# Two-layer gated cross-attention: gathers issued a step earlier, buffers zeroed from SyncE, first loads and last lags rearranged

## What is computed

```python
x = x + tanh(g_xattn[l]) * xattn_l(layernorm(x), layernorm(context), mask)
x = x + tanh(g_ffn[l])   * ffn_l(layernorm(x))
...
# layer 0: 8 heads of 64, keys and values from [context, tokens * kv_gate];
#          ffn: top-2 of 8 experts (sparse mixer), 256 -> 512 (gated SiLU) -> 256
# layer 1: 16 heads of 64; ffn: 8-bit rows and ternary weights, 256 -> 1024,
#          depthwise convolution over the tokens (3 taps), SiLU, 1024 -> 256
```

## Time and profile before

| | |
|---|---|
| median of 3 runs | 1635.83 us (1631.14 to 1636.08) |
| profiled execution: its own time, its span | 1635.99 us, 1634.2 us |
| mean granted clock of TensorE | 0.922 of full speed |
| busy share of the span: PE, DVE, ACT, POOL | 80%, 64%, 60%, 68% |
| moved by DMA | 239.96 MB, mean 147 GB/s |

### The profile page before, as it was taken

How to read it: one execution, slowest core, us unless ns; L and a number is a source line. 1 busy time by engine, 2 the same in 40 slices (tenths; PEclk the granted TensorE clock), 3 DMA queues, 4 the chain that set the end, 5 groups by cost and what they waited for, 6 DMA issues and landing times.

```text
span 1634.2 us, 45130 instructions
## 1 busy us (share of the span) xinstructions
PE 1312.6 (80%) x16918; PEld 1009.1 (62%) x16918; DVE 1045.9 (64%) x2819; ACT 987.9 (60%) x2319; POOL 1118.1 (68%) x1365
## 2 busy tenths in 40 slices
PE   1568778768878978879989998888879888888962
PEld 0346555547767766647878786666656666666651
DVE  4368777886556656855656666667666766676753
ACT  2468776655546666654646567667657766776741
POOL 3567876786657765484757677676767676767765
PEclk9788898989989989999999999999999999999975
DMA  4899897387999944377999994353444335434420
GB/s 136 248 173 231 232 188 207 77 213 160 245 217 248 227 88 85 84 195 194 231 239 224 246 252 94 88 92 66 88 88 87 71 88 88 89 68 88 82 50 6
DMA packets 443129, 239.96 MB, mean 147 GB/s; under 512 B 388784, under 2 KB 425760, under 8 KB 434336
## 3 DMA queue, kind: packets, MB, share of 16 engines
q1 hardware_dynamic: 407100, 172.49, 50.8%
q10 hardware_dynamic: 32740, 57.24, 11.5%
q0 software_dynamic: 3072, 7.34, 1.5%
HBM read 107.78 MB, written 35.50 MB: 88 GB/s over the span
## 4 chain that ended last, share of the span: by engine, by line
PE 35%; POOL 21%; DVE 14%; DMA 11%; issue 9%; ACT 3%; SPq 3%; DVEq 2%; ACTq 1%; POOLq 0%
PE bank_ring L1051 9%; POOL probs L623 6%; PE bank_scores L1011 5%; PE bank_out L1070 5%; PE bank_ring L1089 4%; DMA probs_turned<-probs 4%; DMA raw_weights<-moe_results,route_slots 3%; DVE scores L1299 3%; DVE keys L1311 3%; DMA expert_up<-experts_up 3%; PE bank_ring L1037 3%; PE bank_x L1103 2%; PE bank_x L1150 2%; POOL context L683 2%; POOL moe_rows L642 2%
## 5 line engine op out<-in xcount | busy, mean ns | idle before, releaser
L623 POOL TENSOR_TENSOR probs<-scores,probs 112x487 f16<-112x487 f32 x384 | 431.1, 1138 | 298.9 <-ACT probs L822 291.9
L1299 DVE CUSTOM_DVE_ANT_0 scores<-bank_scores,mask 112x487 f32<-112x487 f32 x384 | 239.5, 661 | 216.4 <-PE bank_scores L1011 208.4
L815 ACT ACTIVATE scores<-scores,score_min 112x487 f32<-112x487 f32 x384 | 265.6, 693 | 85.0 <-DVE score_min L1299 81.2
L842 ACT ACTIVATE values<-bank_ring 128x512 f16<-128x512 f32 x192 | 113.8, 593 | 210.2 <-PE bank_out L1070 168.8
L822 ACT ACTIVATE probs<-scores 112x487 f16<-112x487 f32 x384 | 214.2, 604 | 30.3 <-DMA probs_turned<-probs 14.6
L1051 PE MATMUL bank_ring<-weights,kv_B 128*128 128x128 f16 x3072 | 206.6, 227 | 16.1 <-DVE keys L1311 15.4
L1051 PEld LDWEIGHTS bank_ring<-weights,kv_B 128*128 128x128 f16 x3072 | 191.4, 102 | 35.8 <-DVE keys L1311 32.9
L1070 PE MATMUL bank_out<-values,probs_turned 128*128 128x64 f16 x4608 | 177.0, 197 | 30.0 <-issue 15.9
L1070 PEld LDWEIGHTS bank_out<-values,probs_turned 128*128 128x128 f16 x4608 | 164.5, 101 | 34.2 <-issue 19.4
L1316 DVE SCALAR_TENSOR_TENSOR values<-bank_ring,values 128x512 f16<-128x512 f32 x192 | 131.2, 683 | 78.6 <-ACT values L842 78.4
L1037 PE MATMUL bank_ring<-kv_B,weights 128*128 128x488 f16 x768 | 179.1, 369 | 0.4 <-issue 0.4
(11 more groups left out here) (226 smaller groups left out, 2459.1 us busy)
## 6 DMA issues: line engine op xcount, KB each, us to landing
expert_up<-experts_up SPq DMA_DIRECT2D x43, 1024.0 KB
expert_down<-experts_down SPq DMA_DIRECT2D x43, 512.0 KB
raw_weights<-in_weights ACTq DMA_DIRECT2D x8, 1536.0 KB, 10.9
experts_up<-expert_up ACTq DMA_DIRECT2D x8, 1024.0 KB, 4.9
raw_weights<-in_weights ACTq DMA_DIRECT2D x6, 1024.0 KB, 6.4
probs_turned<-probs SPq DMA_TRANSPOSE x384
context_turned_B<-kv_B ACTq DMA_DIRECT2D x16, 375.0 KB, 7.5
kv_B<-context_turned_B ACTq DMA_DIRECT2D x16, 375.0 KB, 4.5
```

The costliest lines, as they stand in the source:

```text
L623: pool.tensor_tensor(PR[:, u % 4, 1, 0:KEYS], S[:, u % 4, 0:KEYS], PR[:, u % 4, 0, 0:KEYS], ALU.subtract).then_inc(probs_split, 1)
L815: act_e.activation(S[:, u % 4, 0:KEYS], S[:, u % 4, 0:KEYS], ACT.Exp, bias=rmin[:, u % 4:u % 4 + 1], scale=-1.0, accum_out=rsum[:, g % 2, ...
L842: act_e.activation(vN[:, j % 2, 0], bank("v", j)[:].rearrange("p (t d) -> p t d", t=4), ACT.Copy, scale=1 / WSCALE).then_inc(v_hi, 1)
L1299: dve.tensor_tensor_reduce(out=S[:, u % 4, 0:KEYS], in0=bS[u % 2][0:TOK, 0:KEYS], in1=mask[:, m, 0:KEYS], scale=1.0, scalar=3.0e38, op0=AL ...
```

## The change

1. `gather(n)` is issued two steps before its `combine`, not one, for all but n = 0 and n = 6.
2. The zeroing moves from ScalarE (step 0) to SyncE (at the start): five DMAs with runs of 5 to 10 KB, from `moe_rows` in SBUF, which VectorE now clears whole. The loads of expert weights move from step 0 to step -3.
3. Context 1 and tokens 1 are loaded by SyncE behind the first six loads; the wait ahead of the load of the other tokens is gone. On VectorE the wait for the gates moves behind `p_apply(0)`, and the eight `split_chunk` from steps -9, -8 to -6, -5.
4. In layer 0 ScalarE rounds the context a step earlier; GpSimd makes the low half of its first part before both `split_probs` of the step, that of its second between them. For n = 0 the layer-1 halves come behind `kv_ready`.
5. The feed-forward steps of sequences 13 to 15 are packed closer, and in the last half of sequence 15 VectorE takes the two taps, the scaling and the rounding beside GpSimd.

The places of the low halves of keys and values behind the masks (L1311, L1316) do not change.

```diff
+ZERO_DMAS = sum(-(-t // XR_SLOTS) for t in TILES)
...
+F_STEPS = {"stats": 13, "rstd": 14, "rows": 15, "round": 16, "turn": 16, "up0": 17, "up1": 18, "sides0": 19,
+           "sides1": 20, "tanh0": 19, "tanh1": 20, "act0": 20, "act1": 21, "max0": 20, "max1": 21, "rate": 22,
+           "scale0": 23, "scale1": 24, "down": 26, "store": 27}
+LAST_HALF = (NSEQ - 1, 1)
+F_QUICK = {"stats": 13, "rstd": 13, "rows": 13, "round": 13, "turn": 13, "up0": 14, "up1": 15, "sides0": 16,
+           "sides1": 17, "tanh0": 16, "tanh1": 17, "act0": 17, "act1": 18, "max0": 17, "max1": 18, "rate": 19,
+           "scale0": 20, "scale1": 21, "down": 22, "store": 23}
...
+def f_step(n, name):
+    return start_b(n) + (F_QUICK if n >= NSEQ - 2 else F_MIDDLE if n == NSEQ - 3 else F_STEPS)[name]
...
@@ sync
-            sp.wait_ge(x_loaded, 16)
-            sp.dma_start(X[:, 1:NSEQ], x_in[1:NSEQ].rearrange("n t d -> t n d")).then_inc(x_loaded, 16)
+            sp.dma_start(ctxb[0:CP, 1], ctx_in[1].rearrange("(t p) d -> p t d", p=CP)).then_inc(ctx_loaded[1], 16)
+            sp.dma_start(X[:, 1], x_in[1]).then_inc(x_loaded[1], 16)
+            sp.dma_start(X[:, 2:NSEQ], x_in[2:NSEQ].rearrange("n t d -> t n d")).then_inc(x_loaded[2], 16)
+            sp.wait_ge(zeros_set, 1)
+            for b in range(2):
+                rows = xs[b].rearrange("(p t) c -> p (t c)", p=128)
+                for at in range(0, TILES[b] * 2 * DIM, XR_SLOTS * 2 * DIM):
+                    n = min(XR_SLOTS * 2 * DIM, TILES[b] * 2 * DIM - at)
+                    sp.dma_start(rows[:, at:at + n], xr[:].rearrange("p s c -> p (s c)")[:, 0:n])\
+                        .then_inc(rows_zeroed, 16)
...
@@ gpsimd
+                if (j + 4) % 4 == 0 and 0 < (j + 4) // 4 < NSEQ:
+                    split_context((j + 4) // 4, 0, 0)
+                if j == -5:
+                    split_context(0, 0, 0)
+                    split_context(0, 1, 0)
+                    split_latents(0, 0)
+                    split_context(0, 0, 1)
+                    split_context(0, 1, 1)
...
                 if is_pair(j):
                     split_probs(2 * j)
...
-                if (j + 4) % 4 == 0 and 0 <= (j + 4) // 4 < NSEQ:
-                    split_context((j + 4) // 4, 0, 0)
+                if (j + 4) % 4 == 0 and 0 < (j + 4) // 4 < NSEQ:
+                    split_context((j + 4) // 4, 1, 0)
                 if is_pair(j):
                     split_probs(2 * j + 1)
-                if (j + 4) % 4 == 0 and 0 <= (j + 4) // 4 < NSEQ:
-                    split_context((j + 4) // 4, 1, 0)
...
-                    if j == combine_step(n) - 1:
+                    if j == combine_step(n) - (1 if n in (BATCHES[0][0], BATCHES[1][0]) else 2):
                         gather(n)
...
@@ scalar
-                if j == 0:
+                if j == -3:
                     act_e.wait_ge(l0_split, L0_CHUNKS)
                     load_raw(2, 0, 6, weights_in, L0_CHUNKS)
                     load_raw(3, 1, 6, weights_in, L0_CHUNKS + MOE_CHUNKS)
-                    act_e.wait_ge(zeros_set, 1)
-                    for b in range(2):
-                        act_e.dma_start(xs[b].rearrange("(t p) c -> p t c", p=128),
-                                        xr[:, XR_SLOTS - 1:XR_SLOTS, :].to_broadcast([128, TILES[b], 2 * DIM]))\
-                            .then_inc(rows_zeroed, 16)
...
-                if j == FIRST_STEP:
-                    load_context(1)
...
+                if (j + 5) % 4 == 0 and 0 <= (j + 5) // 4 < NSEQ:
+                    round_context((j + 5) // 4)
...
@@ vector
-            dve.memset(xr[:, XR_SLOTS - 1], 0.0)
+            dve.memset(xr[:], 0.0)
...
-                if -9 <= j < -7:
-                    for c in range(4 * (j + 9), 4 * (j + 10)):
+                if -6 <= j < -4:
+                    for c in range(4 * (j + 6), 4 * (j + 7)):
                         split_chunk(c)
...
+                    if (n, 1) == LAST_HALF and j == f_step(n, "sides1"):
+                        conv_sides(n, 1)
...
+                    if (n, 1) == LAST_HALF and j == f_step(n, "scale0"):
+                        f_scale(n, 1)
```

130 lines of the change are left out of this document (83 added, 47 removed).

## The result

| | before | with the change |
|---|---|---|
| median of the runs | 1635.95 us (1631.14 to 1638.04, 4 runs) | **1560.62 us** (1556.74 to 1562.03, 4 runs) |
| profiled execution: time, span | 1635.99, 1634.2 us | 1561.87, 1560.1 us |
| mean granted clock | 0.922 | 0.943 |
| busy PE, DVE, ACT, POOL | 80%, 64%, 60%, 68% | 82%, 68%, 63%, 72% |

What follows compares the result with a forecast made beforehand. Bound by VectorE's gather waits with TensorE's half clock behind them, waits for `kv_ready`, and the opening. Rounds 50, other gathers 8, context halves 9, opening 21, end 2: 90 us off 1636 gives 1546 us; range 1519 to 1590.

Steps and rivals of the forecast that it cites:

- Bound, rounds: Sequences 7 to 15: the earlier gather removes VectorE's wait and TensorE's half clock; 50 us gained, bounds 31 and 55.
- The other gathers: Gathers outside those nine rounds, mainly in the expert stage: 8 us gained, bounds 2 and 12.
- Context halves: Layer 0: one context part leaves the path to `kv_ready` each time TensorE waits for it; 9 us, bounds 0 and 16.
- Opening: Start to step 8: earlier first query projection, no zeros issued on ScalarE; 21 us gained, bounds 10 and 28.
- 11.5 again gives 31.7: Opening: context 2, issued at about 20, takes 11.5 us like context 1 and lands at 31.7 us.
- rival B: Opening gives little: context 2 needs 8 us more and turns of steps 0 and 1 wait; 8 of 21 left, 1559; 0.15.
- two parts of layer 1 (3.2 us) leave the path: Opening: GpSimd makes sequence 0's layer-0 halves first, so two layer-1 parts no longer delay the first query projection; 3.2 us.
- End: Last sequences: `f_up(15)` 4.5 us late, VectorE's share takes 8.5 off, statistics cost 2; 2 us gained, bounds -5 and 6.
- the statistics, now in the same step as their use, cost the last pairs some 2 us: End: packing statistics and their use into one step costs the last pairs some 2 us.
- A: Rounds: GpSimd takes over the wait, its late low halves delaying mask or sums; 50 becomes 25, time 1571; chance 0.16.
- C: Every round: the gather's issue on GpSimd becomes the bound; with 8 us each 1650, slower than before; chance 0.03.
- D: Gathers: the change does not do what it says, the gather still late behind the `combine` before it; no chance given.

Runs made afterwards that it cites:

- g_dose: The changed kernel with two idle GpSimd operations of 1.1 us each behind every gather of sequences 7 to 15: 1582.4 us (0.9646).
- z_small: The changed kernel with the zeros issued by SyncE at the same place, but as two DMAs in runs of 1 KB: 1556.5 us (0.952).
- z_old: The changed kernel with the zeroing back on ScalarE in step 0, in its old form, all else as in the change: 1561.2 us (0.9551).
- t_undo: The changed kernel with old step numbers for all feed-forward parts and GpSimd alone on taps, scaling and rounding of the last half: 1551.1 us (0.9458).
- z_late: The changed kernel with SyncE waiting for context 2 before it issues the zeros: 1561.5 us (0.9564).

## Why the prediction was right, and where it was wrong

**Bound, rounds: right.** The wait, its second half at low clock, and their joint price of 6 us per round were read from the earlier trace rows, and 50 us became 47.3 (49.5 and 48.4 by the two runs that set the gather alone). GpSimd's room was rightly called nearly none: `g_dose`. What was missing is that the `combine` does not stay at 1.05 us: it takes 2.42 to 2.44 in eight of the nine rounds, and 2.56 in one. By that the mask is 0.6 us late, and the step takes 7.34 us instead of the 6.72 of the last sequence: 5.6 us in nine rounds. The 0.4 us per round that I took off for GpSimd's crowding stand for another cause, and came near it by luck. The other 1.8 us are of part 5, in the last round. 9 times the mean before, 12.80, less 6.72 is 54.7; less 5.6 and 1.8 that is 47.3.

**The other gathers: right.** 10.8 against 8 forecast, and by the two runs 7.9 and 9.3; over the twelve profiled executions with the early gather the stretch took 394.5 to 401.8 us, so the sizes are not better known than that.

**Context halves: right in kind; the size is met in part by luck.** 10.8 against 9, in a stretch that scatters by 20 us; the wait for `kv_ready` fell by 9.8 (31.7 to 21.9), not below 20 as I had said it would.

**Opening: the step that failed is "11.5 again gives 31.7".** I priced the load of context 2 by that of context 1, which had run beside the tokens. Beside the zeros in large pieces it took 21.8 us. The rule of the Trainium skill that I set against the change ("DMA: Bandwidth & Descriptors", "Queues, rings and completion order") said so, and I had weighted it as the lesser case (rival B, 0.15): B's first half came, context 2 was 10.4 us later than I gave it, but its second half, that the turns of steps 0 and 1 wait too, did not, so 14.3 of 21 us are left and not 8. My own sign of being wrong, context 2 later than 36 us, was there. The 11.5 us were no evidence on this point: the tokens beside which context 1 ran move in packets of 1 KB, as it does itself. A second step was wrong and is hidden in the change: "two parts of layer 1 (3.2 us) leave the path". With context 2 at 30.9 (`z_small`) the first query projection comes at 35.98 and not at 33.5, for VectorE's copy still waits for the first of the two, behind layer-0 parts that had become 4 us longer (`z_old`). That `z_small` has step 0 at 40.6 and step 8 at 100.1, near the 39 and 101 of the forecast, is right in size and not in the chain.

**End: the step that failed is "the statistics, now in the same step as their use, cost the last pairs some 2 us".** The packed steps cost the last pairs 9.4 (27.3 against 17.8 in `t_undo`; 8.7 against the kernel before). I counted the length of the chain, and not what is queued behind its waits: GpSimd's low halves of that step, TensorE's scores of the next, and half clock on top. That `f_up(15)` would be late was right: 5.3 us against 4.5 (from step 191 on 41.9, in the kernel before 36.6). Of the 8.5 us that VectorE's share was to give behind it, 4.9 came. So 8.5 less 4.5 less 2 became 4.9 less 5.3 less 8.7. Scaling and rounding gave 3.5 of 3.9 (7.7 to 4.24 us), but the taps only 1.5 of 4.6, in part since in VectorE's own order `f_act` of the first half stands behind them:

```profile
1538.91 4.28 DVE L1561 SCALAR_TENSOR_TENSOR context<-raw_weights,vectors,context 128x112 f32<-128x112 f32 x8 [1.66 <-ACT context L951]
1543.11 0.62 DVE L1575 SCALAR_TENSOR_TENSOR context<-raw_weights,context 128x448 f32<-128x448 f32 x1
```

GpSimd had the taps of the first half at 1541.67 and ScalarE its tanh at 1542.28; the 0.8 us up to 1543.11 are VectorE's. The `f_act` of the second half has its input from ScalarE at 1543.80 and begins at 1545.60, behind the maximum of the first half (1544.99), which waits for TensorE: 1.8 us more.

**Rivals.** A did not happen, but is less than a microsecond away. C is excluded: one DMA of a gather takes 1.011 us to issue on the mean of 32, and took 1.014 before (with 14 gathers moved, not the 13 of C's sum). VectorE now works beside it, and the starving of descriptors that the Trainium skill describes ("SBUF — State Buffer", "SBUF: two separate sides") is not seen. The Trainium skill has it for VectorE operations in a mode that takes both ports; no row tells whether any of those beside the issue did, so this is no test of it. D is excluded by the wait itself, 7.3 us instead of 56.4.

**Noise.** I took 5 us for what a measurement tells from no change. The unaltered change, measured again, came out 10 us higher (1570.6).

## What to carry to other kernels

Here a late transfer in a periodic schedule cost its wait and then a stretch at half clock: it showed as a slow stretch behind the wait, and it went with one condition, since the engine that issues earlier had just that much room. In `g_dose`, with 2 us less room, both parts of the price came back in six rounds of nine. When steps are packed closer, do not add up the chain but list, on each engine, what is queued behind each of its waits. And of a bulk transfer moved ahead of the first loads, ask for the size of its pieces: a load of 375 KB that took at most 7.5 us with no zeros beside it (`z_late`, `z_old`) took 21.8 beside 5.5 MB in large pieces and 10.7 beside the same in small ones, and when the large ones were issued later, the next issue on ScalarE took 10.55 us instead. Small pieces are not free either: in `z_small` the next issue on SyncE, a mask, took 14.47 us, which did no harm there.
